# A token-mixing and feed-forward kernel on one Trainium2 core: the loop over supertiles written out, and the token sums moved to VectorE

## The reference

```python
kv = ctx * ctx
r_t = 0.9 * r_(t-1) + kv_t                 # along the tokens of a batch
x = x + layernorm(x) * r
h = layernorm(x) @ W_exp + b_exp           # 512 -> 2048
h = butterfly(h, up_weights, 2048)         # 11 linear stages
h = gelu(h + up_bias)
h = butterfly(h, down_weights, 2048)
x = x + h @ W_con + b_con + down_bias      # 2048 -> 512
```

## Time and profile before

| | us |
|---|---|
| median of 3 runs | 2840.04 (2839.41 to 2841.48) |
| profiled execution | 2842.1 |
| its span | 2840.3 |
| PE matmul busy | 2759.7 (97%) |
| VectorE busy | 2122.4 (75%) |
| ScalarE busy | 1144.7 (40%) |
| GpSimd busy | 548.5 (19%) |

### The profile page before, as it was taken

One profiled execution on the slowest core, in us unless ns is written; L12 is line 12 of the kernel. 1 busy time (PEld: TensorE's weight loads), 2 busy tenths in 40 slices (PEclk: granted clock), 3 DMA queues, 4 the chain that ended last, 5 costly groups with the idle time before them and its releaser, 6 DMA issues.

```text
span 2840.3 us, 40901 instructions
## 1 busy us (share of the span) xinstructions
PE 2759.7 (97%) x12281; PEld 2278.4 (80%) x12281; DVE 2122.4 (75%) x3508; ACT 1144.7 (40%) x1690; POOL 548.5 (19%) x628
## 2 busy tenths in 40 slices
PE   7859999999999999999999999999999999999998
PEld 6838888888888888888888888888888888888887
DVE  7868778787877878787787868777787867778533
ACT  6743433434344343433334343433434344343432
POOL 4531202112120111212011121211112121112100
PEclk8879999999999999999999999999999999999999
DMA  8596575756757585675758567575856757585543
GB/s 204 162 322 186 161 230 152 227 173 187 216 165 222 152 234 166 197 206 160 227 153 245 166 188 202 176 211 154 248 163 198 203 162 215 160 239 163 175 152 100
DMA packets 294011, 541.27 MB, mean 191 GB/s; under 512 B 38718, under 2 KB 102366, under 8 KB 276854
## 3 DMA queue, kind: packets, MB, share of 16 engines
q1 hardware_dynamic: 287382, 534.80, 64.0%
q0 software_dynamic: 1520, 2.27, 0.4%
q10 hardware_dynamic: 4848, 1.13, 0.3%
HBM read 447.89 MB, written 56.62 MB: 178 GB/s over the span
## 4 chain that ended last, share of the span: by engine, by line
PE 92%; DVE 3%; SPq 1%; issue 1%; DMA 1%; ACT 1%; POOL 0%; DVEq 0%; ACTq 0%
PE ps L1498 42%; PE ps L1516 24%; PE ps L1529 24%; PE ps L1359 1%; DMA HX<-in_L_ffn_up_weights_dram 1%; DVE glo L1227 1%; DVE xop L1103 1%; ACT W1f L760 0%; SPq L452 0%; DVE w1r L1017 0%; PE ps L1409 0%; DMA w1r<-w_products 0%; PE ps L1398 0%; SPq L431 0%; SPq L458 0%
## 5 line engine op out<-in xcount | busy, mean ns | idle before, releaser
L1498 PE MATMUL ps<-xop,w1r 128*128 128x512 f32 x5376 | 1367.1, 390 | 28.4 <-DVE xop L1103 10.0
L1498 PEld LDWEIGHTS ps<-xop,w1r 128*128 128x128 f32 x5376 | 1008.6, 188 | 245.5 <-issue 25.0
L1516 PE MATMUL ps<-w2r,ghi 128*128 128x512 f32 x2048 | 630.5, 389 | 0.0
L1529 PE MATMUL ps<-w2r,ghi 128*128 128x512 f32 x2032 | 626.4, 390 | 0.0
L873 ACT ACTIVATE st<-ps 128x512 f32<-128x512 f32 x384 | 229.2, 597 | 861.9 <-PE ps L1498 860.9
L1204 DVE TENSOR_TENSOR x<-ps,x 128x512 f32<-128x512 f32 x508 | 347.9, 685 | 285.2 <-PE ps L1529 284.5
L1516 PEld LDWEIGHTS ps<-w2r,ghi 128*128 128x128 f32 x2048 | 384.5, 188 | 79.8
L1529 PEld LDWEIGHTS ps<-w2r,ghi 128*128 128x128 f32 x2032 | 382.0, 188 | 79.3
L1227 DVE TENSOR_TENSOR glo<-g,ghi 128x512 fp32r<-128x512 f32 x510 | 378.1, 761 | 87.6 <-ACT ghi L891 87.6
L1222 DVE TENSOR_TENSOR g<-ps,st 128x512 f32<-128x512 f32 x384 | 262.7, 684 | 239.6 <-PE ps L1498 235.2
L877 ACT ACTIVATE g<-g,gelu_bias 128x512 f32<-128x512 f32 x384 | 275.5, 717 | 382.6 <-DVE g L1222 382.6
(11 more groups left out here) (141 smaller groups left out, 1708.9 us busy)
## 6 DMA issues: line engine op xcount, KB each, us to landing
w1r<-w_products SPq DMA_DIRECT2D x889, 256.0 KB, 3.5
w2r<-w_split SPq DMA_DIRECT2D x128, 1024.0 KB, 5.0
x<-in_x_dram SPq DMA_DIRECT2D x128, 256.0 KB, 6.9
raw<-kv SPq DMA_DIRECT2D x496, 64.0 KB, 2.1
out_dram<-x SPq DMA_DIRECT2D x120, 256.0 KB, 3.8
kv<-in_ctx_dram SPq DMA_DIRECT2D x64, 256.0 KB, 6.0
raw<-in_ctx_dram SPq DMA_DIRECT2D x64, 256.0 KB, 4.9
w_split<-w2s SPq DMA_DIRECT2D x12, 512.0 KB, 3.4
```

Source lines behind the costliest of these rows:

```text
L1498: last = nc.tensor.matmul(bank[:, :], w1r[:, slot, w, c * P:(c + 1) * P], xop[:, XPOS[m], v, c, :], start=(opens and i == 0), stop=(i == l ...
L1516: last = nc.tensor.matmul(ps_ya[j][:, :], g[:, p % 2, q, j * P:(j + 1) * P], w2r[:, p % 2, kk, w, :], start=(p == 0 and kk == 0 and i == 0 ...
L1529: last = nc.tensor.matmul(ps_yb[:, :], g[:, p % 2, q, j * P:(j + 1) * P], w2r[:, p % 2, kk, w, :], start=(kk == 0 and i == 0), stop=(kk == ...
```

## The change

`supers` and GpSimd's loop call the body for u = 1 to 15 with numbers, so that all sixteen supertiles stand in a row in every instruction stream. `token_sums` is removed from GpSimd. `first_sum(i)` becomes `token_sum(u, i, first)` and is called by VectorE in all supertiles: sums 0 and 1 around `tokens_lo(u+1, 1)` in step 7, sum 2 behind `tokens_lo(u+1, 3)` at the end of step 7, sum 3 in step 0 of the next supertile, behind `tokens_lo(u, 2)`.

```diff
@@ -263,10 +263,8 @@
 
         def supers(eng, body):
             body(0, 0, first=True, last=False)
-            with eng.Fori(1, U - 2, 2) as u:
-                body(u, 1, first=False, last=False)
-                body(u + 1, 0, first=False, last=False)
-            body(U - 1, (U - 1) % 2, first=False, last=True)
+            for u in range(1, U):
+                body(u, u % 2, first=False, last=(u == U - 1))
 
         FOLD = [("WT", k, "dve" if k % 2 and not KH // 4 < k < KH // 2 - 1 else "act") for k in range(KH)]
         FOLD += [("low_up", k, "act") for k in range(KH)]
@@ -657,20 +655,6 @@
                 pool.wait_ge(wsum_ready, 4 * n + 3)
                 nc.gpsimd.tensor_tensor(out=s4, in0=a12, in1=s2, op=ALU.subtract).then_inc(wsum_ready, 1)
 
-            def token_sums(u):
-                r11, r12 = raw[:, 0, 0:2, :], raw[:, 1, 0:2, :]
-                r21, r22 = raw[:, 0, 2:4, :], raw[:, 1, 2:4, :]
-                for i in range(4):
-                    if i == 0:
-                        pool.wait_ge(xT_moved[1], moved_by(u))
-                        pool.wait_ge(xlo_ready, u * NM + 1)
-                    if i in (1, 3):
-                        pool.wait_ge(xsum_ready, u * 4 + i)
-                    if i == 2:
-                        pool.wait_ge(xlo_ready, u * NM + (XPOS[3] + 1))
-                    out, a, b = ((r11, r12, r11), (r12, r22, r12), (r11, r22, r11), (r21, r21, r11))[i]
-                    nc.gpsimd.tensor_tensor(out=out, in0=a, in1=b, op=ALU.subtract).then_inc(xsum_ready, 1)
-
             def first_moves(h):
                 if h == 0:
                     pool.wait_ge(low_matrix_ready, 2)
@@ -728,12 +712,9 @@
                     rstd_rows(u * 2 + h)
                     rstd_gated(u * 2 + h)
                     add_bias(u * 2 + h, h, x)
-                token_sums(u)
-
-            with pool.Fori(1, U - 2, 2) as u:
-                body(u, xs[1])
-                body(u + 1, xs[0])
-            body(U - 1, xs[(U - 1) % 2])
+
+            for u in range(1, U):
+                body(u, xs[u % 2])
             end = U - 1
             pool.wait_ge(ya_out, U * J)
             for g in range(G):
@@ -1103,19 +1084,18 @@
                 nc.vector.tensor_tensor(out=xop[:, XPOS[m], 1, :, :], in0=x_source(m),
                                         in1=xop[:, XPOS[m], 0, :, :].bitcast(f32), op=ALU.subtract).then_inc(xlo_ready, 1)
 
-
-            def first_sum(i):
+            def token_sum(u, i, first=False):
                 r11, r12 = raw[:, 0, 0:2, :], raw[:, 1, 0:2, :]
                 r21, r22 = raw[:, 0, 2:4, :], raw[:, 1, 2:4, :]
                 if i == 0:
-                    dve.wait_ge(first_moved[1], FIRST_MOVES * NX)
-                    dve.wait_ge(xT_moved[1], moved_by(0))
-                    dve.wait_ge(xlo_ready, 1)
-                if i in (1, 3):
-                    dve.wait_ge(xsum_ready, i)
+                    if first:
+                        dve.wait_ge(first_moved[1], FIRST_MOVES * NX)
+                    dve.wait_ge(xT_moved[1], moved_by(u))
+                    dve.wait_ge(xlo_ready, u * NM + 1)
+                if i in (1, 2, 3):
+                    dve.wait_ge(xsum_ready, u * 4 + i)
                 if i == 2:
-                    dve.wait_ge(xsum_ready, 2)
-                    dve.wait_ge(xlo_ready, XPOS[3] + 1)
+                    dve.wait_ge(xlo_ready, u * NM + (XPOS[3] + 1))
                 out, a, b = ((r11, r12, r11), (r12, r22, r12), (r11, r22, r11), (r21, r21, r11))[i]
                 nc.vector.tensor_tensor(out=out, in0=a, in1=b, op=ALU.subtract).then_inc(xsum_ready, 1)
 
@@ -1174,16 +1154,16 @@
             tokens_lo(0, 0)
             tokens_lo(0, 1)
             weights_lo(5)
-            first_sum(0)
-            first_sum(1)
+            token_sum(0, 0, first=True)
+            token_sum(0, 1, first=True)
             for k in range(4):
                 fold_step("low_dn", k)
             weights_lo(6)
             for k in range(4, 8):
                 fold_step("low_dn", k)
             tokens_lo(0, 3)
-            first_sum(2)
-            first_sum(3)
+            token_sum(0, 2, first=True)
+            token_sum(0, 3, first=True)
             weights_lo(7)
             for k in range(8, KH):
                 fold_step("low_dn", k)
@@ -1238,6 +1218,7 @@
                     if old:
                         tokens_lo(u, 5)
                         tokens_lo(u, 2)
+                        token_sum(u, 3)
                     if p == 1 and not first:
                         finish_a(u - 1, nxt, 2)
                         finish_a(u - 1, nxt, 3)
@@ -1290,7 +1271,9 @@
                     if go and p == 6:
                         normalise(u + 1, 1, nxt, 2)
                     if go and p == 7:
+                        token_sum(u + 1, 0)
                         tokens_lo(u + 1, 1)
+                        token_sum(u + 1, 1)
                     block_sum(p, 2, ps_c, 1, 5)
                     low_part(p, 1)
                     take_b(p - 1, 2)
@@ -1312,6 +1295,7 @@
                         normalise(u + 1, 1, nxt, 3)
                     if go and p == 7:
                         tokens_lo(u + 1, 3)
+                        token_sum(u + 1, 2)
 
             supers(dve, body)
             end = U - 1
```

## The result

The kernel after takes 2818.34 us (median of 6 runs, 2817.23 to 2819.25) against 2839.89 us for the one before (6 runs, 2837.66 to 2842.26): the ratio is 0.9921, with a 95% interval of 0.9911 to 0.9931. That is 21.6 us less, where 22 were forecast, at 2818.

A forecast was written before the change was run, and what follows sets the result against it. PE bounds the kernel, busy 97%. Loop pauses 10.2 us and `xop` waits 12.4, at most 22.9 by the ruler, less about 1 allowed: 22 us off the median 2840.04, 2818 us, own range 2815.5 to 2822.

The forecast's parts named there:

- The ceiling of 22.9 us, from the ruler: Steady part, 15 supertile edges: 2470.87 us against 2448.0 for gapless matmul slots; the most it can give.
- Steps (a) and (b): GpSimd's sums go, returning VectorE 1.41 and 2.22 us a supertile; four sums on VectorE cost 1.135 us each.
- rival 1: VectorE's stretches are not GpSimd's doing and stay, sums come on top: 3.0 us an edge, 2862 us; chance 0.05.
- Step (c): VectorE's new order replayed at one edge: all in time, last `down_b` slot 0.2 us to spare, third product 0.5.
- The allowance of 1 us for B3: Last `down_b` slot before an edge, thin margin: 0.05 to 0.1 us an edge, about 1 us in all.
- Step (e): Loops out on all five queues: PE's six "issue" pauses go, 10.2 us taken, bounds 0 to 10.2.
- 12.4 for the `xop` waits: Nine edges inside the loop body, third product late for VectorE: 10.0 us idle plus refilling, 12.4 us.
- rival 4: Removing the loops does nothing, pauses move to page changes of straight code: 12.4 us won, about 2828; chance 0.05.
- Rivals 2 and 3: VectorE sums cost the prologue's 1.87 us, 2838, chance 0.04; third product's wait stays at 15 edges, 2838, chance 0.04.
- the chain's 92% for PE: Profile's chain of waits: 92% of what ended last is matmul, in the three steady lines.

The follow-up runs named there:

- Run 5: Kernel after plus, per supertile on GpSimd with nothing waiting for them, four subtractions: 2865.0 us; or twelve memsets instead: 2817.0 us.
- run 3: Kernel after with the loop put back on VectorE, ScalarE, GpSimd and SyncE but not PE: 2827.06 us; on PE alone: 2838.93 us.
- run 6: Kernel after with one more 128x1024 subtraction a supertile on VectorE, behind token sum 1: 2828.65 us.
- run 1: Kernel before with all sixteen supertiles written out on every engine, token sums left on GpSimd: 2840.07 us, ratio 0.9997.
- run 2: Kernel after with the supertile loop put back on every engine, token sums kept on VectorE: 2841.11 us, ratio 0.9999.

## Why the prediction was right

- *The ceiling of 22.9 us, from the ruler.* Right: 2448.00 of 2448.00 us.
- *Steps (a) and (b), GpSimd's port and the price of a sum.* Right; the median of a sum is 1220 ns, and the stretches vanished with GpSimd's sums. Run 5 makes a world like rival 1's: priced at 3.0 us an edge and 2862, it measured 2865, 3.1 an edge in the trace, in part by luck, since B3 lost less and P2 and B0 more than in the replay.
- *Step (c), the replay.* The times are right within 0.16 us at both ends, on the safe side: `block_sum` comes 0.15 us sooner against PE, 0.67 us into VectorE's idle time where it was 0.82. That is the loop registers: in run 3 take_b(6,2) ends at T - 1.91 where VectorE has the loop and PE has not, just as replayed, and at T - 2.06 where PE has it and VectorE has not. B3's margin was put too small. The replay had 0.2 us and run 6 finds 0.64, because B3 can start 0.06 us behind take_b's end, not 0.13 and a matmul for its weights. The allowance of 1 us for B3 was not needed.
- *Step (e), the loops.* Right in the sum, wrong as a price. I booked 10.2 us for the loop and 12.4 for the `xop` waits, as two terms that add. That the loop alone brings nothing was said and holds (run 1). That the sums alone bring nothing either (run 2) was not seen: 12 us were expected of them. The pause is not a constant: it is the rest of a 3.9 to 4.6 us delay behind B3's wait, and the sums delay that wait. The step also lists the loops of SyncE, ScalarE and GpSimd as hidden and leaves VectorE's out; with PE's written out the other engines' loops still cost 9 us (run 3). That all of them went together was what the sum needed. Both terms are only worth something together. For this change it made no difference, since a pause that is removed is worth the same however it would have grown; rival 4, in which the pauses stay, was priced at 2828 and would have been nearer to 2840 (run 2's 2841, PE's loop alone 2839).
- *Rivals 2 and 3* fell: no prologue price for a sum, no wait left at P2.
- *A reading:* of the chain's 92% for PE the three steady lines hold 90, not all; nothing hangs on it.

## What to carry to other kernels

Lay the bottleneck engine's slots against a ruler first; the 22.9 us were known before any cause was. Then replay the helper engine's queue instruction by instruction against the slots' due times: what counts is the margin at each wait (0.64 us before B3 here), not the 76% of busy time. Two stalls that end at the same edge do not add, and each can hide the other's removal: try the edits together before dropping either.

## What the runs showed of the hardware

- A hardware loop's edge on PE took 3.9 to 4.6 us from the end of take_b, the last wait ahead of the branch, to the first matmul behind it, with one 16 KB packet of PE's instruction queue in between; work already issued hid part of it. In the four kernels measured it left 0.7 to 2.5 us of idle time.
- An idle PE of 2.1 to 2.5 us was followed, at four of six edges in each of two kernels, by 0.50 of granted clock for about two slots; the twelve pauses of 0.7 to 1.7 us in the two others were not.
- A wait of VectorE for PE answered 0.15 us sooner with a constant than with a value worked out from a loop register (take_b(6,2) at T - 2.06 and T - 1.91).
- A GpSimd subtraction beside a VectorE instruction with two SBUF inputs stretched the latter by up to 2.2 us; memsets over the same time by nothing. A VectorE instruction with one input in PSUM was not stretched.
- The instruction queues carried less without the loops, not more (packets, MB, share): before, 114 and 147 packets.

```profile
q8 instruction: 100, 1.64, 0.2%
q14 instruction: 74, 0.61, 0.1%
```
